# Causal softmax attention: scores from three float32r products of split queries and keys, and the weighted values moved ahead of the scores

## The chip, the cores and the metric

The kernel runs on one core of one Trainium2 chip. The metric is the device time of one execution in microseconds (us); lower is better. The engines of the core are named as the profile names them: PE (TensorE, the matmuls; PEld are its weight loads), DVE (VectorE), ACT (ScalarE), POOL (GpSimd) and SP (SyncE, which here only issues DMAs). Each engine has its own instruction stream and takes it in order; engines meet through semaphores.

## The reference, cut to what matters

Input x has 8 batches of 1024 tokens with 256 features. Four blocks follow one another, each with a layernorm in front and a residual around it: softmax attention, a feed-forward block, linear attention, the feed-forward block again. The change is in the first one alone:

```python
q = frac_rope(einsum('btm,mhd->bhtd', x, wq)) * D_HEAD ** (-0.5)   # 2 heads of 128
k = frac_rope(einsum('btm,mhd->bhtd', x, wk)) * D_HEAD ** (-0.5)
v = einsum('btm,mhd->bhtd', x, wv)
s = einsum('bhid,bhjd->bhij', q, k) - NEG * (i < j)
p = softmax(s, axis=-1)
o = einsum('bhij,bhjd->bhid', p, v)
return einsum('bhid,hdm->bim', o, wo)
```

`frac_rope` rotates the first 64 of the 128 features of a head (x times cos plus its swapped halves times sin) and leaves the others.

## The kernel before, in words

The attention phase (function `attention_phase`, from line 436) runs one batch after the other; `turn` of each engine is one batch. A batch is 8 blocks of 128 query rows and 2 heads, so 16 steps; step n works on block i = n // 2 and head h = n % 2, and its keys are the (i + 1) x 128 tokens up to the diagonal.

Number formats. A matmul with plain float32 operands is what the scores (line 832) and the weighted values (line 861) use; each such matmul shows in the trace as two MATMUL records. The projections (lines 322 and 331) and the output projection (line 872) use split operands: a float32r high part (a rounded copy) and a float32r low part (the rest), and three products of parts in place of one product.

The start of a batch. PE projects queries and keys for two halves of 512 tokens, m = 0 to 7 (line 322; m counts half, then query or key, then head). For each m, DVE multiplies by the cosine (`times_cos`, line 705) and ACT copies the swapped halves (`swap_halves`, line 648, two instructions). After every second m DVE multiplies the swapped copy by the sine (`times_sin`, line 712), and POOL adds the two (line 568). The rotary features of both heads lie so that POOL works on 64 partitions at a time; in the first half it does the first 128 tokens and the other 384 apart, queries and then keys. `first_rotated` counts the 128-token pieces, `rotated` the whole halves.

The 16 steps. `scores(n)` multiplies the block's queries with its keys in pieces of up to 512 keys and adds the causal mask on the diagonal (line 835). DVE takes the row maximum (`row_max`, line 722). ACT takes the exponentials (`exp_step`, line 622). PE transposes them in blocks of 128 x 128 (`transpose_probs`, line 850), ACT copies the transposes to SBUF (`evacuate_probs`, line 632), PE multiplies them with the values (`weighted_values`, line 861) into one PSUM bank O, ACT copies O rounded to float32r (`evacuate_out`, line 639), DVE writes the low part (`out_low`, line 717), PE projects (`out_projection`, line 872), DVE adds the result to x (`residual`, line 735). PE also projects the values of one block of 128 tokens at a time (`values`, line 331), which ACT copies (line 660).

The order of the work is written out by hand, one list for each engine. PE at step n: transposes of n, scores of n + 2, value projection of block n + 3, weighted values of n - 1, output projection of n - 2. ACT at step n: exponentials of n + 1, copies of the transposes of n, copy of the value block n + 3, copy of O of n - 1. DVE at step n: reciprocal of n, row maximum of n + 2, low part of O of n - 1, residual of n - 2, and at some steps a piece of the layernorm of the next batch (statistics at 4 and 6, line 131; normalising at 9 and 11, line 155). At steps 14 and 15, which have no scores n + 2, PE transposes the next batch's normalised input in eight matmuls (line 199), and DVE writes its low part (line 209).

There is one bank O. So `weighted_values(n)` waits until `out_low(n - 1)` has read it:

```python
pe.wait_ge(o_lo_done.sem, o_lo_done.at(b, n))      # line 859: n low parts written in this batch
```

Of the kernel before, what the change touches and what calls it, by code (L numbers as in the profile page):

```python
# [21 lines left out]
P = 128  # L22
NB, T, M = 8, 1024, 256
KT = M // P
# [411 lines left out]
def attention_phase(nc, block, sems, env, io, following, fronts, later):  # L436
# [6 lines left out]
    with ExitStack() as ctx:  # L443
# [18 lines left out]
        qk = sb("qk", [P, 2, HA, T])  # L462

        wqkv_raw = qk[:].rearrange("p s h t -> p (s h t)")[:, 0:KT * (WQK + HA * DA)].rearrange("p (k n) -> p k n", k=KT)
        swapped = sb("swapped", [P, NHALF * 2, UN])
        V = sb("v_a", [P, TB, HA * DA])

        steps = [(i, h) for i in range(TB) for h in range(HA)]
        NS = len(steps)
        prob = sb("prob", [P, 2, T])  # L470
        probT = sb("probT", [P, 2, TB, P])
# [4 lines left out]
        wo_raw = prob[:, 0, 0:HA * M].rearrange("p (h m) -> p h m", h=HA)  # L476
# [16 lines left out]
        rotated, first_rotated = sig("a_rotated", 2 * NHALF), sig("a_first_rotated", 2)  # L493
        v_ready, v_done = sig("a_v_ready", TB), sig("a_v_done", TB)
# [10 lines left out]
        def run_batches(eng, turn):  # L505
            turn(0, True, False)
            with eng.Fori(0, NB - 2) as p:
                turn(p + 1, False, False)
            turn(NB - 1, False, True)

# [36 lines left out]
        def _(pool):  # L547
            open_signals(pool, rotated, first_rotated)
# [6 lines left out]
            def turn(b, first, last):  # L555
# [5 lines left out]
                for half in range(NHALF):  # L561
                    for s in range(2):
                        pool.wait_ge(sin_done.sem, sin_done.at(b, 2 * half + s + 1))
                        for some in (slice(0, P), slice(P, UN)) if half == 0 else (slice(0, UN),):
                            for h in range(HA):
                                rows = slice(h * ROT, (h + 1) * ROT)
                                to = qk[rows, s, h, half * UN + some.start:half * UN + some.stop]
# [24 lines left out]
        def _(act):  # L592
# [3 lines left out]
            open_signals(act, swap_done, v_done, p_done, pt_done, o_hi_done)  # L596
# [53 lines left out]

            def square(part):
# [10 lines left out]
            def turn(b, first, last):  # L662
                for m in range(NPROJ - 1):
                    swap_halves(b, m)
                exp_step(b, 0)
                values(b, 0)
                swap_halves(b, NPROJ - 1)
                values(b, 1)
                for n in range(NS):
                    if n + 1 < NS:  # L670
                        exp_step(b, n + 1)
                    evacuate_probs(b, n)
                    if n == 0:
                        values(b, 2)
# [17 lines left out]
        def _(dve):  # L692
            for s in sx:
                s.dve_open(dve)
            open_signals(dve, cos_done, sin_done, o_lo_done, max_done, inv_done, y_done)
# [4 lines left out]
            def times_cos(b, m):  # L700
# [4 lines left out]
                nc.vector.tensor_tensor(qk[:, s, h, at], PS[:, PROJ_RING[m % 4], :], cos[:, h, at],  # L705
                                        ALU.mult).then_inc(cos_done.sem, 1)

            def times_sin(b, k):
# [4 lines left out]
                                        ALU.mult).then_inc(sin_done.sem, 1)  # L713

# [23 lines left out]
            def turn(b, first, last):  # L738
# [5 lines left out]
                for m in range(NPROJ):  # L744
# [5 lines left out]
                    if m == 1 and not first:  # L750
                        residual(b, -1)
                    if m % HA == 0 and m > 0:
                        times_sin(b, m // HA - 1)
                row_max(b, 0)
                row_max(b, 1)
                times_sin(b, NPROJ // HA - 1)
                for n in range(NS):
# [9 lines left out]
                    if not last:  # L767
# [3 lines left out]
                        if n in (9, 11):  # L771
                            ln.dve_normalise(dve, b + 1, (n - 9) // 2)
                    if n == 4 and last:
                        following.ln.dve_normalise(dve, 0)
# [41 lines left out]
        def _(pe):  # L816
# [4 lines left out]
            def scores(b, n):  # L821
                i, h = steps[n]
                if n == 0:
                    pe.wait_ge(first_rotated.sem, first_rotated.at(b, 2))
                elif n == HA or n == HA * UT:
                    pe.wait_ge(rotated.sem, rotated.at(b, 2 * (i // UT + 1)))
                keys = (i + 1) * P
                for c in range(0, keys, UN):
# [3 lines left out]
                    last = nc.tensor.matmul(bank[:, 0:w], qk[:, 0, h, i * P:(i + 1) * P], qk[:, 1, h, c:c + w],  # L832
                                            start=True, stop=not diag)
# [41 lines left out]
            def turn(b, first, last):  # L875
# [998 lines left out]
```

## Time and profile before

| | |
|---|---|
| time, median of 3 runs (lowest, highest) | 1889.74 us (1888.9, 1890.17) |
| span of the profiled execution | 1886.0 us |
| PE busy | 1843.9 us, 98% |
| DVE, ACT, POOL busy | 1395.0, 881.7, 589.6 us |

The profiled execution's own time is not listed beside its span. The span goes from the first to the last instruction, so the time is the span and a little around it: the median stands 3.74 us above the span. The busy time of PE counts overlapping records, so it says that PE was hardly ever without a matmul in flight, and not how fast it went; the distance from the start of one matmul to the start of the next says that. Attention takes the first 540 us of the span or so.

### The profile page before, as it was taken

The numbers are of one execution on the slowest core, as the hardware profiler recorded it, in microseconds if no ns is written. First come the engines' busy times: TensorE is split into PE (matmuls) and PEld (weight loads), VectorE is DVE, ScalarE is ACT, GpSimd is POOL, SyncE is SP. The second block draws the span as 40 slices with busy tenths as digits, with TensorE's granted clock in tenths as the row PEclk, the third lists the DMA queues.
The fourth block names the chain that finished last, engine by engine and source line by source line (L and its number), as shares of the span: only waits on it lengthen the run. The fifth ranks groups of instructions, "written<-read, shape, count | busy, mean of one in ns | idle before, by whom it ended". The sixth has DMA issues, their size and how long they took to land.

```text
span 1886.0 us, 36455 instructions
## 1 busy us (share of the span) xinstructions
PE 1843.9 (98%) x12481; PEld 1541.7 (82%) x12481; DVE 1395.0 (74%) x2679; ACT 881.7 (47%) x1717; POOL 589.6 (31%) x526
## 2 busy tenths in 40 slices
PE   8999999999999999999999999999999998999998
PEld 7888888888888888878787888788878877888887
DVE  6566566556668888777777878787878788888885
ACT  6656656665554444453333333333333332444443
POOL 5313203311332222233433333333333334522211
PEclk9999999999999999999999999999999999999999
DMA  7100000000022122120000000000000001222322
GB/s 246 43 1 0 0 0 0 0 0 0 13 54 54 29 33 32 29 62 13 13 12 12 11 11 11 11 11 11 11 11 11 12 12 20 38 62 62 65 55 58
DMA packets 230630, 53.19 MB, mean 28 GB/s; under 512 B 209696, under 2 KB 228768, under 8 KB 230176
## 3 DMA queue, kind: packets, MB, share of 16 engines
q1 hardware_dynamic: 229296, 49.53, 13.0%
q10 hardware_dynamic: 1264, 2.76, 0.4%
q8 instruction: 40, 0.66, 0.1%
q14 instruction: 30, 0.25, 0.0%
HBM read 18.69 MB, written 8.39 MB: 14 GB/s over the span
## 4 chain that ended last, share of the span: by engine, by line
PE 74%; DVE 9%; issue 6%; POOL 4%; SPq 2%; ACT 2%; DMA 1%; DVEq 0%; ACTq 0%; POOLq 0%
PE PS L1203 16%; PE PS L1212 9%; PE PS L322 8%; PE PS L331 7%; PE PS L861 7%; PE PS L832 6%; PE PS L850 3%; PE PS L1732 3%; PE PS L1706 3%; PE PS L1668 3%; SPq L270 2%; PE PS L1711 2%; PE PS L1721 2%; PE PS L872 2%; DVE lin_zq L1504 2%
## 5 line engine op out<-in xcount | busy, mean ns | idle before, releaser
L322 PE MATMUL PS<-ln_xh,lin_w 128*128 128x512 f32 x768 | 249.9, 394 | 9.2 <-POOL ln_xl L280 5.4
L1135 ACT ACTIVATE ff_silu<-PS 128x512 f32<-128x512 f32 x192 | 114.4, 597 | 232.9 <-PE PS L1203 204.5
L1170 DVE SCALAR_TENSOR_TENSOR ff_h<-PS,ff_silu 128x512 f32<-128x512 f32 x192 | 131.2, 684 | 107.7 <-PE PS L1203 94.1
L322 PEld LDWEIGHTS PS<-ln_xh,lin_w 128*128 128x128 f32 x768 | 144.3, 188 | 47.6 <-DVE lin_kT L1487 8.6
L568 POOL TENSOR_TENSOR qk<-qk,swapped 64x128 f32<-64x128 f32 (+2 forms) x96 | 96.9, 1009 | 240.2 <-DVE swapped L712 234.4
L1154 DVE TENSOR_TENSOR ff_h_lo<-ff_h,ff_h_hi 128x512 fp32r<-128x512 f32 x192 | 165.1, 860 | 0.4
L861 PE MATMUL PS<-probT,v_a 128*128 128x128 f32 x1152 | 153.3, 278 | 0.0
L861 PEld LDWEIGHTS PS<-probT,v_a 128*128 128x128 f32 x1152 | 139.5, 192 | 14.3 <-ACT probT L632 7.4
L322 PE MATMUL PS<-ln_xl,lin_w 128*128 128x512 f32 x384 | 150.2, 391 | 0.0
L832 PE MATMUL PS<-qk 128*128 128x512 f32 (+3 forms) x384 | 145.2, 489 | 1.0 <-POOL qk L568 0.9
L722 DVE TENSOR_REDUCE neg_max<-PS 128x1 f32<-128x256 f32 (+7 forms) x128 | 95.6, 752 | 62.3 <-PE PS L835 60.9
L166 POOL TENSOR_SCALAR ln_var_eps<-ln_mean_var 128x4 f32<-128x4 f32 x64 | 15.5, 242 | 402.7 <-DVE ln_mean_var L139 402.7
L1442 ACT ACTIVATE lin_yg_hi<-stage 128x512 fp32r<-128x512 f32 x64 | 40.3, 630 | 205.3 <-DVE stage L1550 135.1
L1121 ACT ACTIVATE ff_h_hi<-ff_h 128x512 fp32r<-128x512 f32 x192 | 119.5, 622 | 9.3 <-DVE ff_h L1170 9.3
L1418 POOL TENSOR_TENSOR lin_state<-lin_state,lin_decay_c 128x512 f32<-128x512 f32 x48 | 50.0, 1042 | 233.9 <-PE PS L1711 233.9
L1362 POOL TENSOR_TENSOR lin_qsT<-lin_qT,lin_decay_q 128x512 f32<-128x512 f32 x64 | 99.2, 1566 | 65.8 <-DVE lin_qT L1487 56.1
L1424 POOL TENSOR_TENSOR lin_yg_lo<-stage,lin_yg_hi 128x512 fp32r<-128x512 f32 x64 | 82.1, 1282 | 107.3 <-ACT lin_yg_hi L1442 107.3
L1457 ACT ACTIVATE ln_xn<-PS 128x512 f32<-128x512 f32 x128 | 76.6, 598 | 65.8 <-PE PS L322 56.7
L622 ACT ACTIVATE prob<-PS,neg_max 128x256 f32<-128x256 f32 (+7 forms) x128 | 94.4, 738 | 14.1 <-DVE neg_max L722 10.5
L1212 PE MATMUL PS<-ff_w_hi,ff_h_hi 128*128 128x256 f32 x384 | 97.7, 288 | 1.6 <-issue 1.4
L1212 PE MATMUL PS<-lin_w,ff_h_hi 128*128 128x256 f32 x384 | 97.6, 287 | 1.6 <-issue 1.5
L639 ACT ACTIVATE oT_hi<-PS 128x128 fp32r<-128x128 f32 x128 | 35.5, 277 | 135.1 <-PE PS L861 134.1
(190 smaller groups left out, 5354.2 us busy)
## 6 DMA issues: line engine op xcount, KB each, us to landing
ff_raw<-ln_xn SPq DMA_DIRECT2D x464, 32.0 KB, 2.0
ln_xl<-ln_xn SPq DMA_DIRECT2D x288, 32.0 KB, 2.0
out_x<-X SPq DMA_DIRECT2D x15, 512.0 KB, 2.9
X<-in_x SPq DMA_DIRECT2D x7, 1024.0 KB, 5.5
stage<-in_w_lin SPq DMA_DIRECT2D x1, 2048.0 KB, 8.1
stage<-in_w_gate SPq DMA_DIRECT2D x2, 768.0 KB, 7.4
stage<-in_w_up SPq DMA_DIRECT2D x2, 768.0 KB, 8.8
stage<-in_w_down SPq DMA_DIRECT2D x2, 768.0 KB, 10.2
```

The source lines that it names most:

```text
L322: last = nc.tensor.matmul(out, w, x, start=n == 0, stop=n == len(terms) - 1)
L331: last = nc.tensor.matmul(out, x[:, at], w, start=n == 0, stop=n == len(terms) - 1)
L568: done = nc.gpsimd.tensor_tensor(to, to, swapped[rows, 2 * half + s, some], ALU.add)
L832: last = nc.tensor.matmul(bank[:, 0:w], qk[:, 0, h, i * P:(i + 1) * P], qk[:, 1, h, c:c + w], start=True, stop=not diag)
L861: last = nc.tensor.matmul(O, V[:, j, h * DA:(h + 1) * DA], probT[:, n % 2, j, :], start=j == 0, stop=j == i)
L1121: nc.scalar.activation(h_hi[:, slot(par, f), :], h[:, f % 2, :], ACT.Copy).then_inc(hi_done.sem, 1)
L1135: nc.scalar.activation(silu[:, f % NB_GU, :], PS[:, f % NB_GU, :], ACT.Silu, scale=W_SCALE).then_inc(silu_done.sem, 1)
L1154: nc.vector.tensor_tensor(h_lo[:, slot(par, f), :], h[:, f % 2, :], h_hi[:, slot(par, f), :].bitcast(F32), ALU.subtract).then_inc(lo_done. ...
L1170: nc.vector.scalar_tensor_tensor(h[:, f % 2, :], PS[:, NB_GU + f % NB_GU, :], W_SCALE, silu[:, f % NB_GU, :], ALU.mult, ALU.mult).then_inc ...
L1203: ins = nc.tensor.matmul(PS[:, bank, :], w, x, start=n == 0, stop=n == len(parts) - 1)
L1212: ins = nc.tensor.matmul(Y[:, t // 2, (t % 2) * M:(t % 2 + 1) * M], a[:, slot(par, f), t * P:(t + 1) * P], w[:, f % NF, :], start=f == 0 a ...
L1362: nc.gpsimd.tensor_tensor(qsT[:, j, :].rearrange("p (c t) -> p c t", t=P), qT[:, j, :].rearrange("p (c t) -> p c t", t=P), Gq[:, j, :].uns ...
```

## The change

Queries and keys, once rotated, are split: ACT writes a float32r copy (`qk_hi`), DVE or POOL the float32r rest (`qk_lo`). Each piece of the scores is three float32r products in place of one float32 product. The work is cut by tokens: the first 128 of the first half (FIRST; low parts on DVE), its other 384 (REST; low part of the queries on POOL, of the keys on DVE), and the second half (WHOLE; both low parts on POOL). PE's list changes its order in two places: the first value projection comes ahead of the first two scores, and in each step the weighted values of n - 1 and the value projection come ahead of the scores of n + 2. To have room, the unsplit queries and keys live in the buffers of the probabilities and of the normalised input, and raw weights are loaded into the value buffer.

```diff
+        qk_hi, qk_lo = sb("qk_hi", [P, 2, HA, T], F32R), sb("qk_lo", [P, 2, HA, T], F32R)
+        qk = [prob[:].rearrange("p s (h t) -> p s h t", h=HA),
+              env["norm"].xn[:].rearrange("p t m -> p (t m)").rearrange("p (s h t) -> p s h t", s=2, h=HA)]
+        FIRST, REST, WHOLE = slice(0, P), slice(P, UN), slice(0, UN)
```

POOL, for each half, after its rotations:

```diff
-                pool.wait_ge(rotated.sem, rotated.at(b, 2 * NHALF))
+                    pool.wait_ge(rotated.sem, rotated.at(b, 2 * (half + 1)))
+                    for s in range(2):
+                        if half > 0 or s == 0:
+                            pool.wait_ge(qk_hi_done.sem, qk_hi_done.at(b, 2 * half + s + 1))
+                            some = WHOLE if half > 0 else REST
+                            nc.gpsimd.tensor_tensor(of_tokens(qk_lo, s, half, some), qk[half][:, s, :, some],
+                                                    of_tokens(qk_hi, s, half, some).bitcast(F32),
+                                                    ALU.subtract).then_inc(pool_lo_done.sem, 1)
+                    if half == 0:
+                        pool.wait_ge(pool_lo_done.sem, pool_lo_done.at(b, 1))
```

ACT, the copies and their places in the batch:

```diff
+            def qk_high(b, s, half, some):
+                ready, k, done = (first_rotated, s + 1, first_hi_done) if some == FIRST else (rotated, 2 * half + s + 1, qk_hi_done)
+                act.wait_ge(ready.sem, ready.at(b, k))
+                nc.scalar.activation(of_tokens(qk_hi, s, half, some), qk[half][:, s, :, some], ACT.Copy).then_inc(done.sem, 1)
...
                 for m in range(NPROJ - 1):
                     swap_halves(b, m)
+                    if m == 3:
+                        qk_high(b, 0, 0, FIRST)
+                    if m == 5:
+                        qk_high(b, 1, 0, FIRST)
+                        qk_high(b, 0, 0, REST)
+                values(b, 0)
+                qk_high(b, 1, 0, REST)
                 exp_step(b, 0)
-                values(b, 0)
                 swap_halves(b, NPROJ - 1)
                 values(b, 1)
                 for n in range(NS):
                     if n + 1 < NS:
                         exp_step(b, n + 1)
                     evacuate_probs(b, n)
+                    if n == 1:
+                        for s in range(2):
+                            qk_high(b, s, 1, WHOLE)
```

DVE:

```diff
+            def first_low(b, s):
+                dve.wait_ge(first_hi_done.sem, first_hi_done.at(b, s + 1))
+                nc.vector.tensor_tensor(of_tokens(qk_lo, s, 0, FIRST), qk[0][:, s, :, FIRST],
+                                        of_tokens(qk_hi, s, 0, FIRST).bitcast(F32), ALU.subtract).then_inc(first_lo_done.sem, 1)
...
+                    if m in (5, 6):
+                        first_low(b, m - 5)
...
                 row_max(b, 0)
                 row_max(b, 1)
+                rest_k_low(b)
                 times_sin(b, NPROJ // HA - 1)
...
                         if n in (9, 11):
+                            dve.wait_ge(pool_lo_done.sem, pool_lo_done.at(b, 3))
                             ln.dve_normalise(dve, b + 1, (n - 9) // 2)
```

PE, the waits, the products and the order:

```diff
                 if n == 0:
-                    pe.wait_ge(first_rotated.sem, first_rotated.at(b, 2))
-                elif n == HA or n == HA * UT:
-                    pe.wait_ge(rotated.sem, rotated.at(b, 2 * (i // UT + 1)))
+                    pe.wait_ge(first_lo_done.sem, first_lo_done.at(b, 2))
+                elif n == HA:
+                    pe.wait_ge(pool_lo_done.sem, pool_lo_done.at(b, 1))
+                    pe.wait_ge(rest_k_lo_done.sem, rest_k_lo_done.at(b, 1))
+                elif n == HA * UT:
+                    pe.wait_ge(pool_lo_done.sem, pool_lo_done.at(b, 3))
...
-                    last = nc.tensor.matmul(bank[:, 0:w], qk[:, 0, h, i * P:(i + 1) * P], qk[:, 1, h, c:c + w],
-                                            start=True, stop=not diag)
+                    for k, (q_part, k_part) in enumerate(((qk_hi, qk_hi), (qk_hi, qk_lo), (qk_lo, qk_hi))):
+                        last = nc.tensor.matmul(bank[:, 0:w], q_part[:, 0, h, q], k_part[:, 1, h, c:c + w],
+                                                start=k == 0, stop=k == 2 and not diag)
...
+                values(b, 0)
                 scores(b, 0)
                 scores(b, 1)
-                values(b, 0)
...
                     transpose_probs(b, n)
+                    if n + 2 >= NS and not last:
+                        sx[n + 2 - NS].pe(pe, b + 1, b + 1)
+                    if n >= 1:
+                        weighted_values(b, n - 1)
+                    if n == 0:
+                        values(b, 2)
+                    if n + 3 < TB:
+                        values(b, n + 3)
                     if n + 2 == HA * UT:
                         pe.wait_ge(v_done.sem, v_done.at(b, TB))
                     if n + 2 < NS:
                         scores(b, n + 2)
-                    if n == 0:
-                        values(b, 2)
-                    if n + 3 < TB:
-                        values(b, n + 3)
-                    if n + 2 >= NS and not last:
-                        sx[n + 2 - NS].pe(pe, b + 1, b + 1)
-                    if n >= 1:
-                        weighted_values(b, n - 1)
                     if n >= 2:
                         out_projection(b, n - 2)
```

## Rows read from the trace of the kernel before

**Rows 1.** The page: busy time of each engine; the chain that ended last, by engine.
```profile
PE 1843.9 (98%) x12481; PEld 1541.7 (82%) x12481; DVE 1395.0 (74%) x2679; ACT 881.7 (47%) x1717; POOL 589.6 (31%) x526
...
PE 74%; DVE 9%; issue 6%; POOL 4%; SPq 2%; ACT 2%; DMA 1%; DVEq 0%; ACTq 0%; POOLq 0%
```

**Rows 2.** One batch's stretch: us, busy PE, PEld, DVE, ACT, POOL, then PEclk.
```profile
223.56:289.18 65.62, 65.62 (x441) 55.34 (x440) 40.11 (x103) 39.62 (x99) 14.65 (x17) 1.00 0.00 0
```

**Rows 3.** Timeline of PE: start us, us, line, shapes; a distance between starts is the pace.
```profile
234.69 1.02 PE L832 MATMUL PS<-qk 128*128 128x512 f32 x2
235.55 0.22 PE L835 MATMUL PS<-mask_b,ident_b 128*128 128x128 bf16 x1
...
268.17 1.04 PE L850 MATMUL PS<-ident,prob 128*128 128x128 f32 x8
269.04 1.04 PE L199 MATMUL PS<-ident,ln_xn 128*128 128x128 f32 x8
...
283.74 0.39 PE L322 MATMUL PS<-a_xh,wqkv_hi 128*128 128x512 f32 x1
...
288.96 0.39 PE L322 MATMUL PS<-a_xh,wqkv_lo 128*128 128x512 f32 x1
...
290.08 0.28 PE L331 MATMUL PS<-wqkv_lo,ln_xh 128*128 128x256 f32 x1
290.20 0.28 PE L331 MATMUL PS<-wqkv_hi,ln_xh 128*128 128x256 f32 x1
```

**Rows 4.** Timeline of PE and of DVE late in a batch: mask, maximum, low part.
```profile
266.14 0.22 PE L835 MATMUL PS<-mask_b,ident_b 128*128 128x128 bf16 x1
266.19 1.78 PE L861 MATMUL PS<-probT,v_a 128*128 128x128 f32 x14
267.73 0.36 PE L872 MATMUL PS<-wo_a_hi,oT_hi 128*128 128x256 f32 x1
...
266.40 1.23 DVE L722 TENSOR_REDUCE neg_max<-PS 128x1 f32<-128x1024 f32 x1 [1.80 <-PE PS L835]
268.32 0.29 DVE L717 TENSOR_TENSOR oT_lo<-PS,oT_hi 128x128 fp32r<-128x128 f32 x1 [0.70 <-ACT oT_hi L639]
268.53 0.48 DVE L735 SCALAR_TENSOR_TENSOR X<-PS,row_inv,X 128x256 f32 x1
```

**Rows 5.** Groups by shape, DVE, 90 to 480 us: narrowest and widest maximum used below.
```profile
L722 DVE TENSOR_REDUCE neg_max<-PS 128x1 f32<-128x1024 f32 x12 | 14.7, 1224 | 14.1 <-PE PS L835 14.1
...
L722 DVE TENSOR_REDUCE neg_max<-PS 128x1 f32<-128x384 f32 x12 | 6.7, 558 | 2.1 <-PE PS L835 1.5
```

**Rows 6.** Timeline of PE: a value projection that waited for ACT's copy.
```profile
292.83 0.39 PE L331 MATMUL PS<-wqkv_hi,ln_xh 128*128 128x256 f32 x1
293.05 0.28 PE L331 MATMUL PS<-wqkv_hi,ln_xl 128*128 128x256 f32 x1
```

**Rows 7.** Timeline of POOL (twice, to different ends) and of ACT in a batch's start.
```profile
284.17 7.09 POOL L568 TENSOR_TENSOR qk<-qk,swapped 64x128 f32<-64x128 f32 x8 [37.76 <-DVE swapped L712]
...
284.17 12.82 POOL L568 TENSOR_TENSOR qk<-qk,swapped 64x128 f32<-64x128 f32 x12 [37.76 <-DVE swapped L712]
...
292.39 0.39 ACT L660 ACTIVATE v_a<-PS 128x256 f32<-128x256 f32 x1
...
295.48 0.27 ACT L639 ACTIVATE oT_hi<-PS 128x128 fp32r<-128x128 f32 x1
```

**Rows 8.** Groups by shape, 541 to 800 us: SBUF subtractions and a float32r copy elsewhere.
```profile
L1154 DVE TENSOR_TENSOR ff_h_lo<-ff_h,ff_h_hi 128x512 fp32r<-128x512 f32 x90 | 77.6, 862 | 0.1
...
L280 POOL TENSOR_TENSOR ff_odd_xl<-ff_raw,ff_odd_xh 128x1024 fp32r<-128x1024 f32 x8 | 19.4, 2428 | 43.4 <-ACT ff_odd_xh L275 43.4
...
L275 ACT ACTIVATE ff_odd_xh<-ff_raw 128x1024 fp32r<-128x1024 f32 x8 | 8.5, 1059 | 13.8 <-DMA ff_raw<-ln_xn 11.2 <-PE PS L1203 2.6
```

**Rows 9.** Timeline of PE in the linear attention; a stretch behind it (columns as rows 2).
```profile
838.37 0.88 PE L1678 MATMUL PS<-lin_zq,lin_head_sum 128*32 128x512 f32 x2 [3.44 <-issue]
...
840.00:841.00 1.00, 1.00 (x6) 0.83 (x3) 1.00 (x3) 0.00 (x0) 0.88 (x1) 0.50 0.00 0
```

More of the change, by code:

```diff
@@ L493, in attention_phase @@
         rotated, first_rotated = sig("a_rotated", 2 * NHALF), sig("a_first_rotated", 2)
+        qk_hi_done, first_hi_done = sig("a_qk_hi_done", 2 * NHALF), sig("a_first_hi_done", 2)
+        first_lo_done, rest_k_lo_done = sig("a_first_lo_done", 2), sig("a_rest_k_lo_done", 1)
+        pool_lo_done = sig("a_pool_lo_done", 3)
         v_ready, v_done = sig("a_v_ready", TB), sig("a_v_done", TB)
@@ L509, in run_batches, with of_tokens @@
             turn(NB - 1, False, True)
+        def of_tokens(parts, s, half, some):
+            return parts[:, s, :, half * UN + some.start:half * UN + some.stop]
         def score_rows(n):
@@ L547, in _ @@
         def _(pool):
-            open_signals(pool, rotated, first_rotated)
+            open_signals(pool, rotated, first_rotated, pool_lo_done)
             ln.pool_open(pool)
@@ L566, in turn @@
                                 rows = slice(h * ROT, (h + 1) * ROT)
-                                to = qk[rows, s, h, half * UN + some.start:half * UN + some.stop]
+                                to = qk[half][rows, s, h, some]
                                 done = nc.gpsimd.tensor_tensor(to, to, swapped[rows, 2 * half + s, some], ALU.add)
                             done.then_inc((first_rotated if some.stop == P else rotated).sem, 1)
-                pool.wait_ge(rotated.sem, rotated.at(b, 2 * NHALF))
+                    pool.wait_ge(rotated.sem, rotated.at(b, 2 * (half + 1)))
[8 more added lines that the diff above has]
+                        pool.wait_ge(pool_lo_done.sem, pool_lo_done.at(b, 1))
                 if first:
@@ L694, in _ @@
                 s.dve_open(dve)
-            open_signals(dve, cos_done, sin_done, o_lo_done, max_done, inv_done, y_done)
+            open_signals(dve, cos_done, sin_done, o_lo_done, max_done, inv_done, y_done, first_lo_done, rest_k_lo_done)
             ln.dve_open(dve)
@@ L704, in times_cos @@
                 dve.wait_ge(proj_ready.sem, proj_ready.at(b, m + 1))
-                nc.vector.tensor_tensor(qk[:, s, h, at], PS[:, PROJ_RING[m % 4], :], cos[:, h, at],
+                nc.vector.tensor_tensor(qk[half][:, s, h, :], PS[:, PROJ_RING[m % 4], :], cos[:, h, at],
                                         ALU.mult).then_inc(cos_done.sem, 1)
@@ L713, in times_sin, with rest_k_low @@
                                         ALU.mult).then_inc(sin_done.sem, 1)
+            def first_low(b, s):
+                dve.wait_ge(first_hi_done.sem, first_hi_done.at(b, s + 1))
+                nc.vector.tensor_tensor(of_tokens(qk_lo, s, 0, FIRST), qk[0][:, s, :, FIRST],
+                                        of_tokens(qk_hi, s, 0, FIRST).bitcast(F32), ALU.subtract).then_inc(first_lo_done.sem, 1)
+            def rest_k_low(b):
+                dve.wait_ge(qk_hi_done.sem, qk_hi_done.at(b, 2))
+                nc.vector.tensor_tensor(of_tokens(qk_lo, 1, 0, REST), qk[0][:, 1, :, REST],
+                                        of_tokens(qk_hi, 1, 0, REST).bitcast(F32), ALU.subtract).then_inc(rest_k_lo_done.sem, 1)
             def out_low(b, n):
@@ L1865 @@
     }
-    nc = bacc.Bacc("TRN2", target_bir_lowering=False, num_devices=1)
+    nc = bacc.Bacc("TRN2", target_bir_lowering=False, num_devices=1, dynamic_dma_scratch_size=1024)
     io = {}
```

9 lines of the change are left out of this document (5 added, 4 removed).

## The prediction

> **What bounds the kernel now.** The page comes first: PE is busy 98% of the span, and three quarters of the chain that ended last is PE [rows 1]. That chain is the list of what to shorten, but the busy figure says little of pace. So the second view is the table of stretches, cut from one batch's first scores to the next's: a batch takes 65.62 us, PE is busy in all of it, and neither DVE nor ACT reaches 41 us [rows 2]. The third is PE's timeline, read by the distance between starts: a batch is a dense row of matmuls, each kind at its own pace [rows 3]. In attention, PE's own work is therefore the time, and a microsecond in which PE waits is lost for good. The fourth is the timeline of the other engines, since they decide whether PE waits after the change.
>
> The sum is made against the span of 1886.0 us. The median of the runs is 3.74 us above it, which I take as what lies around the span, and I add the difference to 1889.74. 0.2% (3.8 us) is what a measurement of this kernel can tell from no change.
>
> **Part 1: three float32r products for one float32 product (PE).** A 512-key piece takes 235.55 - 234.69 = 0.86 us now, two records of 0.43. A float32r product of 512 columns takes 0.227: 24 of them stand in a row, the first at 283.74 and the last at 288.96, 23 distances in 5.22 us. One of 256 columns takes 0.12 [rows 3]. A batch has 12 pieces of 512 keys, 4 of 384, 4 of 256 and 4 of 128. Now, in proportion to columns: 0.86 x (12 + 3 + 2 + 1) = 15.5 us. After, with 0.173 for 384 columns (between the two rows): 3 x (12 x 0.227 + 4 x 0.173 + 4 x 0.12 + 4 x p) where p is the price of 128 columns, which no row has in float32r. From below, a quarter of the 512-column pace: 0.057. From above, as much as a whole float32 piece of 128 keys: 0.215. I take 0.11, the pace of the eight transposes, also 128 columns with one weight load each (0.87 / 8) [rows 3]. That gives 13.0 us, a gain of **2.5 us a batch** (1.2 to 3.1).
>
> The Trainium skill, "TensorE: Matmul & The Clock Gate", section "Back-to-back issue gap", gives about 131 ns for a 512-column matmul in a stream with weight loads; by that the gain would be about 3.5 us a batch more. The rows measure 0.227, so the sum keeps that.
>
> **Part 2: the start of a batch.** POOL adds the rotation without a break from 284.17, is through the first half at 291.26 and through the second at 296.99 [rows 7]. The change puts the subtraction for REST of the queries between the halves: 768 columns; the nearest row is 2.43 us for 1024, so 1.8 us [rows 8]. The second half is then rotated at 298.9. ACT, in step 1, waits for exactly this in the copy of WHOLE of the keys, about 1.06 us [rows 8], to 299.9. Behind it in ACT's queue stand the copy of value block 4 (0.39) and the copy of O of step 0 (0.27) [rows 7], to about 300.5; then DVE's low part (0.29 [rows 4]) and PE's restart. Weighted values of step 1 can start at 300.9. Now ACT makes this copy of O at 295.48 [rows 7].
>
> What has PE to do until then? The projections end at 289.19. In the new order come five value blocks (6 x 0.12 each, 3.6), four scores with masks (about 1.8), four transposes (0.44) and the weighted values of step 0 (0.22): 6.0 us, to 295.2. PE loses about **5.6 us a batch** (4.4 if that subtraction goes at DVE's pace [rows 8] and the two small copies are hidden; 6.6 if value block 4 reaches ACT a microsecond late). Smaller waits earlier (ACT's two REST copies push the first exponentials and the value copies back by some 2 us) lie inside this loss.
>
> **Part 3: the order in every step.** Weighted values of n need the low part of O of n - 1. DVE makes it behind the row maximum of n + 2, which waits for the scores of n + 2. Now those scores are followed by weighted values, output projection, transposes and the next scores before the low part is wanted. After the change only an output projection and the transposes of n + 1 lie between. Count from the start of the mask that ends the scores. DVE's maximum starts 0.26 later (266.14 to 266.40). It holds DVE for some 0.07 less than its duration, as the low part does: 0.29 long, and the next instruction starts 0.21 after it. Then comes the low part itself, 0.29 [rows 4]. A PE that waits restarts late: the copy ended at 292.78 [rows 7], the matmul opens at 292.83, and the next follows after 0.22 where 0.12 is usual [rows 6], so 0.15. With a maximum of 0.56 (384 keys, step 2) to 1.22 (1024 keys, step 12) [rows 5] that is 1.19 to 1.85. The cover is 0.05 for the mask (to 266.19), 0.44 for the output projection (267.73 to 268.17), and 0.11 for each transpose, 2 to 7 of them [rows 3, 4]: 0.71 to 1.26. PE waits 0.5 to 0.6 in the even steps and 0.1 less in the odd ones, which have one transpose more: 5.3 us for the 11 steps 2 to 12. In steps 13 and 14 the next batch's transposes cover it. The statistics that DVE does in steps 4 and 6 delay the next maximum; I add 0.4. **5.7 us a batch** (4.2 without the statistics and without the 0.1 by which a restarted PE is slower; 7.5 if every wait is longer by another 0.15, as much as the restart itself).
>
> **Edits that I cost at nothing.** FIRST: DVE's low part of the keys waits for ACT's copy, which waits for POOL's first 128 keys. These are instructions 5 and 6 of the 8 in 7.09 us, so done at about 288.7 [rows 7], and the low part a microsecond later; the first value block, moved there, covers it. If it did not, the loss would be part of part 2's wait. REST of the keys on DVE (768 columns at 0.86 per 512 [rows 8], 1.3 us) stands ahead of the last sine product and delays it by about 2 us; POOL wants that product only after the REST subtraction, and it comes in time. POOL's two WHOLE subtractions (2 x 2.43) end at about 303.8, some 4 us before the scores of step 8 would start now, and DVE's normalising in step 9 is later still. The raw weights are only loaded elsewhere: no DMA moves in its queue, SP's list is as before, and PE's wait for them still precedes the first value block. DVE gains some 2.1 us and ACT 4.5 us of work a batch, against some 25 us of idle time each [rows 2].
>
> **The sum.** -2.5 + 5.6 + 5.7 = +8.8 us a batch, with 8 batches +70: 1889.7 + 70 = **1960 us**. Lowest with all bounds: -3.1 + 4.4 + 4.2 = +5.5, so 1934. Highest: -1.2 + 6.6 + 7.5 = +12.9, so 1993.
>
> **The rivals.**
>
> *The products pay and the queues have slack.* If the low part of O came early enough in every step and the copy of O of step 0 were not late, only part 1 stays: -2.5 x 8 = -20, 1870 us, faster. For it: DVE, ACT and POOL idle a third of a batch or more [rows 2], and PE does not wait for them now. Against it: the place is a queue, not a load; DVE's list still has the maximum first. It decides where the waits add up to less than 2.5 us a batch. 7%.
>
> *One of the two waits is hidden.* With part 2 alone +3.1 a batch, 1914; with part 3 alone +3.2, 1915. For it, each wait rests on one chain of five or six rows. 8%.
>
> *The clock falls.* In the linear attention PE stood 3.44 us, and two microseconds after it had started again the granted clock stood at 0.50, 1.2 in place of 2.4 GHz [rows 9]. In part 2, PE's last wait is about as long, once a batch, if the earlier waits are small. If the clock stays there for as long as PE had stood, 3.4 us at half pace lose 1.7; 8 of them make 1960 + 14 = 1974. The skill's page named above says in "HAM oscillation" that idle gaps between bursts put the clock back to half rate; the row agrees for 3.44 us, and no row shows a shorter wait that did it. 17%.
>
> *The products run at the float32 pace.* Then three of 0.43 replace 0.86 and the scores cost 7.7 us a batch more in place of 2.5 less: about 2045. The projections' rows speak against it [rows 3]. 1%.
>
> **How the numbers follow.** The forecast has 67%, with 1934 to 1993 as its range. The fallen clock lies inside that range, so the range holds 84% as it stands and I leave it. Slower by over 0.2%: 67 + 17 + 8 + 1 = 93%, less 1 for a mixture that ends near zero: 92%. Faster: 6% of the 7 of the first rival; the remaining 2% within 0.2%.
>
> **What would show it right or wrong.** In the profile after: a batch some 9 us longer than 65.62; score records of 512 columns 0.23 apart; PE's weighted values waiting for DVE's low part in most steps, about 0.5 us each, and once a batch for over 3 us; ACT's copy of O of step 0 right behind the copy of WHOLE of the keys, and that one released by POOL. The forecast is wrong if the weighted values start without a wait, if the batch shrinks, or if 128-column products show a pace far from 0.11. Feed-forward and linear attention should not change.

## The result, and the profile after

The changed kernel takes **1994.51 us** (median of 4 runs, 1993.93 to 1996.11), the kernel before 1889.32 us beside it: a ratio of 1.0556, 95% interval [1.0544, 1.0569]. Slower, as forecast (92%); but 1960 us was forecast, and the range ended at 1993. The span of the profiled execution is 1993.3 us, 107.3 above that of before, and its own time 1995.07, 1.8 above its span. So of the 3.74 us that the forecast put around the span, some 2 were the difference between runs; since the forecast adds its change to the median, this moves nothing in it.

The page of the changed kernel answers to [rows 1]: busy time, chain, and the group of weighted values with its idle time.

```profile
PE 1873.9 (94%) x12673; PEld 1587.2 (80%) x12673; DVE 1424.1 (71%) x2703; ACT 921.2 (46%) x1765; POOL 646.1 (32%) x550
...
PE 50%; issue 22%; DVE 12%; POOL 8%; SPq 3%; ACT 2%; DMA 1%; DVEq 0%; ACTq 0%; POOLq 0%
...
L913 PE MATMUL PS<-probT,v_a 128*128 128x128 f32 x1152 | 162.3, 287 | 57.8 <-DVE oT_lo L759 57.7
```

PE's share of the chain fell from 74% to 50%, and one group of matmuls now has 57.8 us of idle time ahead of it, nearly all of it ended by DVE's low part of O. PE's waits from 150 to 480 us (a little over four batches; each line has the total in us, the number of times and the longest) show the pattern: a long one and a dozen short ones in each batch.

```profile
PE PS L913 <- DVE oT_lo L759: 30.7, 51, 3.8
PE PS L902 <- ACT prob L640: 4.2, 4, 1.1
PE PS L331 <- ACT v_a L683: 2.1, 4, 0.5
```

One batch as a stretch, and two single microseconds in it (columns as in [rows 2]):

```profile
338.86:417.34 78.48, 69.30 (x464) 60.82 (x464) 43.74 (x106) 44.63 (x105) 21.67 (x20) 0.96 0.00 0
...
350.00:351.00 1.00, 0.83 (x4) 0.86 (x5) 0.10 (x2) 0.43 (x3) 1.00 (x2) 0.50 0.00 0
...
356.00:357.00 1.00, 1.00 (x9) 0.84 (x9) 0.00 (x0) 0.49 (x2) 0.00 (x0) 0.99 0.00 0
```

A batch takes 78.48 us in place of 65.62 [rows 2], and PE's granted clock is no longer 1.00: it stands at 0.50 (1.2 GHz) for 6.8 us of the batch, from about 1 us before the long wait ends. The first two batches take 77.4 to 77.5, with 3.4 us at 0.50.

**The start of a batch** (projections end at 337.85), PE's timeline, then those of ACT, DVE and POOL:

```profile
341.71 0.33 PE L902 MATMUL PS<-ident,prob 128*128 128x128 f32 x1 [1.06 <-ACT prob L640]
...
343.26 0.39 PE L331 MATMUL PS<-wqkv_hi,ln_xh 128*128 128x256 f32 x1 [0.52 <-ACT v_a L683]
...
350.17 0.77 PE L913 MATMUL PS<-probT,v_a 128*128 128x128 f32 x2 [3.81 <-DVE oT_lo L759]
350.59 0.56 PE L331 MATMUL PS<-wqkv_hi,a_xh 128*128 128x256 f32 x1
350.95 0.41 PE L331 MATMUL PS<-wqkv_hi,a_xl 128*128 128x256 f32 x1
351.16 0.41 PE L331 MATMUL PS<-wqkv_lo,a_xh 128*128 128x256 f32 x1
```

```profile
345.79 1.05 ACT L672 ACTIVATE qk_hi<-ln_xn 128x1024 fp32r<-128x1024 f32 x1
348.21 1.06 ACT L672 ACTIVATE qk_hi<-ln_xn 128x1024 fp32r<-128x1024 f32 x1 [1.36 <-POOL ln_xn L577]
349.17 0.37 ACT L683 ACTIVATE v_a<-PS 128x256 f32<-128x256 f32 x1
349.44 0.27 ACT L657 ACTIVATE oT_hi<-PS 128x128 fp32r<-128x128 f32 x1
...
349.74 0.29 DVE L759 TENSOR_TENSOR oT_lo<-PS,oT_hi 128x128 fp32r<-128x128 f32 x1 [3.13 <-ACT oT_hi L657]
...
332.85 6.81 POOL L577 TENSOR_TENSOR prob<-prob,swapped 64x128 f32<-64x128 f32 x8 [40.18 <-DVE swapped L744]
339.73 2.15 POOL L584 TENSOR_TENSOR qk_lo<-prob,qk_hi 128x768 fp32r<-128x768 f32 x1
342.04 6.13 POOL L577 TENSOR_TENSOR ln_xn<-ln_xn,swapped 64x512 f32<-64x512 f32 x4 [0.16 <-POOL qk_lo L584]
```

This is the forecast chain link by link: POOL ends its rotations at 348.17, ACT's copy of WHOLE of the keys waits for that, the value block and O stand behind it, DVE follows, and PE starts at 350.17, 12.3 after its projections (forecast: 11.7). New is what comes after: a 256-column product goes at 0.21 us (350.95 to 351.16) in place of 0.12 [rows 3].

**A step**, PE's and DVE's timelines at full clock:

```profile
366.03 0.23 PE L887 MATMUL PS<-mask_b,ident_b 128*128 128x128 bf16 x1
...
366.50 0.60 PE L902 MATMUL PS<-ident,prob 128*128 128x128 f32 x4
367.46 1.13 PE L913 MATMUL PS<-probT,v_a 128*128 128x128 f32 x8 [0.36 <-DVE oT_lo L759]
368.35 0.48 PE L884 MATMUL PS<-qk_hi 128*128 128x512 f32 x1
368.66 0.39 PE L884 MATMUL PS<-qk_lo,qk_hi 128*128 128x512 f32 x1
368.89 0.39 PE L884 MATMUL PS<-qk_hi,qk_lo 128*128 128x512 f32 x1
369.12 0.22 PE L884 MATMUL PS<-qk_hi 128*128 128x128 f32 x1
...
366.29 0.82 DVE L764 TENSOR_REDUCE neg_max<-PS 128x1 f32<-128x640 f32 x1 [1.68 <-PE PS L887]
367.03 0.28 DVE L759 TENSOR_TENSOR oT_lo<-PS,oT_hi 128x128 fp32r<-128x128 f32 x1
```

The weighted values wait for a low part that stands behind the row maximum of the scores just made. The bracket says 0.36, counted from the modelled end of the last transpose (367.10). But four transposes at 0.11 [rows 3] let the next matmul start at 366.94, so 0.52 are lost.

**Where the 107.3 us are.** First scores come 1.2 later (27.2 for 26.1); the seven batches from first scores to first scores take 548.8 for 461.4, so 87.4; the last batch, to its last output projection, 10.5; and the three blocks behind the attention 8.5 to their last matmul (0.3 of it comes back behind that), in a dozen places of 0.3 to 1.5 us each.

### The profile page after: what moved, and what is told of

The parts are those of the page before. It is cut to its first block, busy times and chain, and to the rows that moved or that the text cites. A ratio compares the mean times of both kernels' runs of the same rounds, so it can differ in the third digit from the quotient of the medians.

```text
span 1993.3 us, 37046 instructions
## 1 busy us (share of the span) xinstructions
PE 1873.9 (94%) x12673; PEld 1587.2 (80%) x12673; DVE 1424.1 (71%) x2703; ACT 921.2 (46%) x1765; POOL 646.1 (32%) x550
## 3 DMA queue, kind: packets, MB, share of 16 engines
q1 hardware_dynamic: 229296, 49.53, 12.3%
## 4 chain that ended last, share of the span: by engine, by line
PE 50%; issue 22%; DVE 12%; POOL 8%; SPq 3%; ACT 2%; DMA 1%; DVEq 0%; ACTq 0%; POOLq 0%
PE PS L1255 14%; PE PS L1264 8%; PE PS L331 5%; PE PS L322 4%; SPq L270 3%; PE PS L913 3%; PE PS L1784 3%; PE PS L1758 2%; POOL prob L577 2%; PE PS L1763 2%; PE PS L1720 2%; PE PS L884 2%; PE PS L1773 2%; POOL ln_xn L577 2%; DVE ln_stats L131 2%
## 5 line engine op out<-in xcount | busy, mean ns | idle before, releaser
L913 PE MATMUL PS<-probT,v_a 128*128 128x128 f32 x1152 | 162.3, 287 | 57.8 <-DVE oT_lo L759 57.7
L577 POOL TENSOR_TENSOR prob<-prob,swapped 64x128 f32<-64x128 f32 (+1 forms) x64 | 51.0, 797 | 253.5 <-DVE swapped L744 249.9
L155 DVE TENSOR_SCALAR ln_xn<-X,ln_mean_var,ln_rstd 128x256 f32 (+1 forms) x256 | 97.3, 442 | 1.3 <-POOL ln_rstd L169 1.3
L1264 PE MATMUL PS<-ff_w_hi,ff_h_lo 128*128 128x256 f32 x384 | 95.9, 283 | 0.0
```

Of the source, the lines that this page charges most:

```text
L155: last = nc.vector.tensor_scalar(out, x, self.mean_var[:, t, 0:1], self.rstd[:, t:t + 1], ALU.subtract, ALU.mult)
L913: last = nc.tensor.matmul(O, V[:, j, h * DA:(h + 1) * DA], probT[:, n % 2, j, :], start=j == 0, stop=j == i)
L1264: ins = nc.tensor.matmul(Y[:, t // 2, (t % 2) * M:(t % 2 + 1) * M], a[:, slot(par, f), t * P:(t + 1) * P], w[:, f % NF, :], start=f == 0 a ...
```

## The experiments

Each ran beside the kernel before; its time is followed by the ratio to that kernel and the 95% interval. Each expectation, written ahead of its run, names a theory and a rival. Batch times and waits are those of the profiled execution. Unless said otherwise the diff is against the changed kernel.

**order_back: PE's steps in the order of before.**

```diff
                     transpose_probs(b, n)
-                    if n >= 1:
-                        weighted_values(b, n - 1)
...
                         scores(b, n + 2)
...
+                    if n >= 1:
+                        weighted_values(b, n - 1)
```

> The changed kernel with the old order of PE's steps (scores of n + 2 ahead of the value block and the weighted values of n - 1); the splits and all else stay. Theory (three losses: PE waits for the low part of O in every step, 5.5 us a batch; it waits once for 3.8 us at the start; the clock falls after that wait, 3.4 us a batch): the waits of the steps go, and at the start the scores of step 4 and value block 5 fill part of the long wait, so some 2.2 us of it are left. A batch then takes 66.5 to 67.5 us and the kernel 1897 to 1905 if the clock holds, about 1925 to 1930 if the shorter wait still brings it down. Rival (the order costs nothing, the float32r products and the splits do): above 1980, and the weighted values still wait in every step.

1923.09 us, 1.0183 [1.0166, 1.02], 2 us under the range that was given for a fallen clock. Batches with a full clock take 68.2. Its waits from 200 to 480 us, where the clock holds:

```profile
PE PS L913 <- DVE oT_lo L759: 8.5, 4, 2.1
PE PS L902 <- ACT prob L640: 4.3, 4, 1.1
PE PS L884 <- DVE qk_lo L754: 3.2, 4, 0.8
```

The dozen short waits are gone, and so is the fall of the clock in these batches; 10 us of each batch went with the two. Three waits at the start are left. The clock still fell in the first three batches and the last. So the order was the larger part. The first batch still took 75.0, which both_sq below was to mend.

**order_only: the kernel before with the new order alone, float32 scores** (the same lines moved the other way).

> The kernel before with nothing but the new order of PE's steps; scores stay float32, no splits. Theory: every step's weighted values wait for the low part of O behind the row maximum, 5.5 us a batch, and at the start some 1.5 us more; no wait is longer than 1 us, the clock holds. 71.5 to 73.5 us a batch, the kernel 1937 to 1952. Rival (the order is harmless by itself and the waits come from the added splits): 1885 to 1895.

1953.33 us, 1.0344 [1.0325, 1.0363], 1 us above the theory's range; the rival is out. Batches take 73.5, so the order alone loses 7.9. The clock never fell in them.

```profile
PE PS L861 <- DVE oT_lo L717: 16.2, 48, 0.6
PE PS L331 <- ACT v_a L660: 2.2, 4, 0.6
```

**low_first: DVE writes the low part of n - 1 ahead of the row maximum of n + 2.**

```diff
                     inverse(b, n)
+                    if n >= 1:
+                        out_low(b, n - 1)
                     if n + 2 < NS:
                         row_max(b, n + 2)
-                    if n >= 1:
-                        out_low(b, n - 1)
```

> The changed kernel with one swap on DVE: in each step the low part of O of n - 1 comes ahead of the row maximum of n + 2. PE's order stays new, the WHOLE copies stay in step 1. Theory: the waits of the steps come from the low part standing behind the maximum in DVE's queue, so they go (6.5 us a batch), while the long wait at the start and the fall of the clock after it stay: 71 to 73 us a batch, the kernel 1935 to 1952. Rival (the one bank O and PE's new order cause them whatever DVE does): 1985 or more.

1943.33 us, 1.0282 [1.0265, 1.0299]: hit. Batches take 71.8 to 71.9, 6.6 less than in the changed kernel. Up to 1 us of that may be the clock: three of these batches stand at half clock for 3.4 us in place of 6.8, and the changed kernel's batch with 3.4 takes 77.4. The rest, 5.5 or more, shows that it is the place in DVE's list, and neither DVE's load nor its durations, that makes PE wait in the steps.

**whole_late: ACT's two copies of WHOLE in step 3 in place of step 1.**

```diff
-                    if n == 1:
+                    if n == 3:
                         for s in range(2):
                             qk_high(b, s, 1, WHOLE)
```

> The changed kernel with ACT's two WHOLE copies in step 3 in place of step 1; PE's order stays new. Theory: the copy of O of step 0 no longer stands behind POOL, the 3.8 us wait shrinks below 1 us, the granted clock stays at full in the attention, the step waits of about 0.5 us stay. A batch loses 3 us of wait and 3.4 us of slow clock: about 72 us in place of 78.4, the kernel 1940 to 1948. Rival (the clock falls from the many small waits together, or for another reason): the clock still falls once a batch and only the 3 us go, 1965 to 1975.

1969.43 us, 1.0422 [1.0405, 1.044]. Batches take 75.1. The wait of 3.81 shrank to 0.58, which shows that it was ACT's queue; but the gain was 3.3 a batch, and the time lies in the rival's range, because the clock still fell, now only for 3.4 us. PE's waits and one microsecond of a batch:

```profile
410.43 0.32 PE L902 MATMUL PS<-ident,prob 128*128 128x128 f32 x1 [1.06 <-ACT prob L640]
...
411.98 0.42 PE L331 MATMUL PS<-wqkv_hi,ln_xh 128*128 128x256 f32 x1 [0.52 <-ACT v_a L683]
...
412.00:413.00 1.00, 1.00 (x5) 1.00 (x6) 1.00 (x1) 0.72 (x4) 0.94 (x2) 0.59 0.00 0
```

It stands at half already in 412 to 413, right behind two waits of 1.06 and 0.52.

**keep_busy: 30 products that nobody reads, in PE's list ahead of the long wait.**

```diff
+                    if n == 2:
+                        pe.wait_ge(y_done.sem, y_done.at(b, 0))
+                        for _ in range(30):
+                            nc.tensor.matmul(Y, sx[1].hi[:, 0, 0:P], sx[1].hi[:, 0, 0:M], start=True, stop=True)
                     if n >= 1:
                         weighted_values(b, n - 1)
```

> The changed kernel with 30 extra products of 256 columns (0.12 us each, 3.6 us) on PE ahead of the weighted values of step 1, into the bank of the output projection, whose contents nobody reads before it is written anew. Theory: the products fit into the wait of 3.8 us, which ends when it did; but PE does not stand still and the granted clock stays at full, so the 6.8 us at half clock go, 3.4 us a batch: 1966 to 1972. Rival (the clock is no price of its own, or falls anyway): 1990 to 2000, or up to 29 us more if the extra products lie on the path.

1981.04 us, 1.0486 [1.0469, 1.0504]: between the two ranges. The long wait's end, and a batch (columns as in [rows 2]):

```profile
341.52 3.83 PE L965 MATMUL PS<-a_xh 128*128 128x256 f32 x30
345.63 0.46 PE L913 MATMUL PS<-probT,v_a 128*128 128x128 f32 x2 [0.29 <-DVE oT_lo L759]
...
334.25:410.54 76.29, 70.33 (x495) 62.03 (x495) 43.67 (x106) 44.55 (x105) 21.79 (x20) 1.00 0.00 0
```

The weighted values start as late as before (11.4 after the first scores for 11.3), so only the clock differs. Batches without a fall take 76.2 to 76.4, against 78.4 with one of 6.8 us in the changed kernel: **the fall costs 2.0 us a batch**; the kernel gained 13.5. Three of its eight batches still have a fall of 3.4 us, begun ahead of the extra products, and take 76.8 to 77.4. The price is less than the theory had: the fall's first microsecond lies in the wait itself, and PE's slower work is cover for some of the step waits behind it.

**both_sq: order_back and whole_late together, and in the first batch the squares of the feed-forward weights two per step from step 12.**

> The changed kernel with three edits: PE's steps in the old order, the WHOLE copies in step 3, and ACT's squares of the first batch (they check the feed-forward weights) two a step from step 12 on, since POOL now prepares those weights later. Theory: no wait in the steps, no long wait at the start; left are the waits for the first exponentials and for the REST low parts, 2 to 3 us a batch, about as much as the products gain. 65.5 to 66.5 us a batch, the kernel 1886 to 1898; a fall of the clock in some batches adds little. Rival (the float32r scores cost more than the float32 ones): above 1910.

1916.6 us, 1.0145 [1.0128, 1.0162]: missed. Two batches, without and with a fallen clock:

```profile
239.19:305.06 65.87, 63.86 (x465) 58.17 (x465) 44.23 (x106) 43.74 (x105) 21.79 (x20) 1.00 0.00 0
305.06:372.45 67.39, 65.37 (x464) 59.64 (x464) 44.24 (x106) 43.72 (x105) 21.75 (x20) 0.97 0.00 0
```

Batches without a fallen clock take 65.87, 0.2 more than before, but most of them have 3.4 us at half clock and take 67.4. The waits of 1.06 (transposes, for ACT's first exponentials) and 0.81 (scores of step 2, for DVE's low part) stay in each; the same two waits are followed by a fall in some batches and not in others. And the first batch took 76.8.

**late_split: a version meant to win.** It is the kernel before, order and start included; the scores of steps 0 to 7 stay float32, and only those of steps 8 to 15, the long ones, are three products. ACT makes the high parts in steps 2 to 4 and POOL the low parts behind its rotations, so that they are there before step 8 asks for them; ACT's squares stand as in both_sq. As in the changed kernel, buffers are shared anew and `dynamic_dma_scratch_size` is 1024. From the diff against the kernel before, the products:

```diff
+                    if i < UT:
+                        last = nc.tensor.matmul(bank[:, 0:w], qf[:, 0, h, i * P:(i + 1) * P], qf[:, 1, h, c:c + w],
+                                                start=True, stop=not diag)
+                    else:
+                        q = slice((i - UT) * P, (i - UT + 1) * P)
+                        for k, (q_part, k_part) in enumerate(((q_hi, k_hi), (q_hi, k_lo), (q_lo, k_hi))):
```

> A version meant to beat both: PE's order and the start of a batch as in the kernel before, with float32 scores in steps 0 to 7 from a buffer of their own; only steps 8 to 15 use the three float32r products, so the splits (keys of both halves, queries of the second) are made by ACT in steps 2 to 4 and by POOL behind its rotations, before step 8 wants them; the squares as in the run of three edits. Theory: the pieces of steps 8 to 15 gain 1.8 us a batch and nothing waits: 63.6 to 64.2 us a batch, the clock holds, the kernel 1872 to 1880. Rival (any copy in ACT's queue or any work on POOL next to DVE costs PE a wait): 1889 or more.

1885.93 us, 0.998 [0.997, 0.9989]: missed by 6 us. The batches are as expected, 63.83 us, without a wait; the first, 71.99, is not: PE waits 4.8 us there for DVE.

**late_split2: the scales of the next layernorm ahead of POOL's long subtraction** (against late_split). In late_split's first batch DVE's normalising waited for POOL, whose 10 us subtraction of the feed-forward weights stood ahead of the scales that it needs (late_split, DVE):

```profile
61.22 1.38 DVE L155 TENSOR_SCALAR ln_xn<-X,ln_mean_var,ln_rstd 128x256 f32<-128x256 f32 x4 [6.76 <-POOL ln_rstd L169]
```

```diff
-                    nc.gpsimd.tensor_tensor(raw, raw, env["ff_w_hi"][:].bitcast(F32),
-                                            ALU.subtract).then_inc(env["ff_low"], 1)
...
                         ln.pool_rstd(pool, b + 1, half)
+                    if first:
+                        nc.gpsimd.tensor_tensor(raw, raw, env["ff_w_hi"][:].bitcast(F32),
+                                                ALU.subtract).then_inc(env["ff_low"], 1)
```

> The version meant to beat both, with one more edit: in the first batch POOL makes the layernorm's scales for the second batch ahead of its 10 us subtraction on the feed-forward weights, not behind it. Theory: in the run before, the first batch took 72.0 us in place of 63.8, since DVE's normalising in step 9 stood until POOL had come through those weights, and ACT and PE behind it (one wait of 4.8 us on PE). With the scales first that wait goes: the first batch 64 to 65.5 us, the kernel 1875 to 1880. Rival (the first batch's wait comes from the squares on ACT, or from something else): 1884 to 1888 as before.

1886.7 us, 0.9988 [0.9979, 0.9997]: missed; the first batch took 73.5. DVE no longer waits, but one of its rows is long. POOL's and DVE's timelines:

```profile
52.45 9.99 POOL L594 TENSOR_TENSOR stage<-stage,ff_w_hi 128x4608 f32<-128x4608 f32 x1
...
53.86 0.48 DVE L756 SCALAR_TENSOR_TENSOR X<-PS,row_inv,X 128x256 f32<-128x256 f32 x1
54.26 9.31 DVE L155 TENSOR_SCALAR ln_xn<-X,ln_mean_var,ln_rstd 128x256 f32<-128x256 f32 x4
63.49 0.15 DVE L748 RECIPROCAL row_inv<-row_sum 128x1 f32<-128x1 f32 x1
63.56 1.07 DVE L743 TENSOR_REDUCE neg_max<-PS 128x1 f32<-128x896 f32 x1
```

Four normalising instructions, 1.37 us elsewhere, take 9.31 and end 1.1 after POOL's one instruction. The first of them alone takes 8.34, to 62.60, where POOL ends at 62.44; the three others take their usual 0.4 each. So the first stood until POOL was through; DVE's row just before, with a PSUM operand, ran beside POOL in its usual 0.48.

**late_split3: that subtraction in two pieces, each behind a normalising** (against late_split2).

```diff
-                        nc.gpsimd.tensor_tensor(raw, raw, env["ff_w_hi"][:].bitcast(F32),
-                                                ALU.subtract).then_inc(env["ff_low"], 1)
+                        for j, part in enumerate((slice(0, 4 * WPART), slice(4 * WPART, NW))):
+                            pool.wait_ge(ln.ready.sem, ln.ready.at(b + 1, j + 1))
+                            nc.gpsimd.tensor_tensor(raw[:, part], raw[:, part], env["ff_w_hi"][:, part].bitcast(F32),
+                                                    ALU.subtract).then_inc(env["ff_low"], 1)
```

> The late split once more, with GpSimd's one 10 us subtraction of the first batch cut in two pieces (2048 and 2560 columns), each of them issued only when VectorE has normalised half of the next batch's input; ScalarE's squares of the later parts wait for the second piece. Theory (a long GpSimd instruction on SBUF holds up VectorE's normalising, which took 9.31 us beside it instead of 1.37): the four normalising instructions of the first batch are back near 1.4 us in sum, TensorE waits nowhere over 1 us in the first batch, the first batch takes 64 to 66 us and the kernel 1876 to 1880. Rival (the first batch is late for another reason): 1884 to 1888 again, with a wait of over 4 us left in it.

**1878.96 us, 0.9948 [0.9935, 0.9962]: 0.5% faster than the kernel before**, and the theory hit. DVE, POOL, and a stretch as long as a batch:

```profile
55.10 1.37 DVE L155 TENSOR_SCALAR ln_xn<-X,ln_mean_var,ln_rstd 128x256 f32<-128x256 f32 x4
...
56.55 4.57 POOL L596 TENSOR_TENSOR stage<-stage,ff_w_hi 128x2048 f32<-128x2048 f32 x1 [3.26 <-DVE ln_xn L155]
...
62.27 1.37 DVE L155 TENSOR_SCALAR ln_xn<-X,ln_mean_var,ln_rstd 128x256 f32<-128x256 f32 x4
...
63.72 5.67 POOL L596 TENSOR_TENSOR stage<-stage,ff_w_hi 128x2560 f32<-128x2560 f32 x1 [2.60 <-DVE ln_xn L155]
...
221.00:284.83 63.83, 63.83 (x458) 57.44 (x457) 39.96 (x102) 42.16 (x102) 21.69 (x20) 1.00 0.00 0
```

The first batch takes 64.7 and PE's longest wait in it is 0.6. So the products do pay, where PE's order and the start of a batch stay as they were.

## Why the prediction was wrong in its size

Direction and mechanisms held: the likeliest case came about, and all its waits are in the trace at their forecast places; but the fallen clock, which the prediction held to be a rival, came on top of it. The size was short, by terms of different weight. For a batch from the third on, in us:

```text
                         forecast   measured
products (part 1)          -2.5       -1.9
start of a batch (part 2)  +5.6       +6.3
order in the steps (3)     +5.7       +6.4
fallen clock                0         +2.0
sum                        +8.8      +12.8   (78.48 - 65.62 = 12.86)
```

**Part 1: right in pace, 0.6 too high in sum.** Columns go as forecast: 0.23 for 512 (368.66 to 368.89), 0.11 for 128. In order_back, 65.62 + 4.15 of waits (2.13, 1.06, 0.81 and 0.14) + 0.4 for PE's restarts - 68.22 leaves a gain of 1.9. The records agree: counted from start to start, the scores of one of its batches take 14.4 us for 15.6 before, the transposes 7.0 for 7.8 and the masks 0.9 for 0.7. The first of three products often takes 0.31 (368.35 to 368.66), which the sum lacks; but in order_back it also opens 0.03 behind the last transpose in place of 0.11, which gives that back, so the 0.6 lies in no single row. The Trainium skill, "TensorE: Matmul & The Clock Gate", section "Back-to-back issue gap", gives 131 ns for a matmul of 512 columns in a stream. The trace has 0.23, as the projections had it, and the measurement decides.

**Part 2: right, 0.7 short.** Nearly all of it lies with POOL: the REST subtraction took 2.15 for 1.8, the second half's rotation 6.13 for 5.7, with 0.16 of waiting between, less 0.3 in the first half. Behind it the links took 2.0, as forecast. (The 6.3 takes PE's work up to there at the forecast 6.0; the prediction's own 300.9 less 295.2 is 5.7 where it has 5.6.)

**Part 3: right, 0.7 short.** From the mask to DVE's maximum 0.26, as forecast (366.03 to 366.29); the low part ends at 367.31. Then the restart: the matmul opens 0.15 later, where the forecast had 0.05, and in order_only the records of the weighted values take 16.45 a batch for 15.34, 0.09 for each of 12 waits. So a restart costs 0.24, not 0.15: one microsecond a batch. Step 14, which was thought covered, waits as well (0.17). The 6.4 is order_only's 7.9 less the waits that belong to the start there (0.55 and 0.58, with their restarts about 1.5). The prediction's upper bound of 7.5 is 7.4 by its own counting, since eleven waits longer by 0.15 add 1.65.

**The clock: this is the step that failed.** The forecast has a wait "about as long" as the 3.44 us of [rows 9] in each batch, behind which that row shows the clock at 0.50, and yet makes the fall a rival of 17%. On the forecast's own numbers it belonged in the sum, where it stood at nothing; the runs show 2.0 us a batch. The rival's price of 14 us for the kernel came close to keep_busy's 13.5, in part by luck: it has 3.4 us at half pace and all of it lost, the trace has 6.8 of which a part costs nothing. The ground for doubt, that earlier waits might make the last one short, had no row behind it; whole_late shows that even without it the clock falls. With those 14 us in the sum, the forecast is 1974 and its range ends at 2007. The range as stated was passed by 1.5 us only: without the fall, or without the 8.5 us behind the attention, the time would have lain inside it.

**Edits costed at nothing.** FIRST was nearly hidden in the steady batches (a wait of 0.14 ahead of the first scores; 1.54 in the last batch, where the kernel before waits 0.91), the waits of 1.06 and 0.52 lie inside part 2's loss, as the prediction said, and SP's list played no part (PE's one wait for a DMA is 4.8 us at the very start, 4.9 in the kernel before). That feed-forward and linear attention do not change was wrong by 8.5 us in the profiled run. order_back has 6.4 there, late_split3 2.6, and order_only, whose buffers and number formats are those of before, 2.3; no experiment was made on it, and its cause stays open.

**The rivals.** Slack in the queues is out (order_only, order_back); one hidden wait is out, since undoing either part gains (order_back, whole_late); products at the float32 pace are out. Products at the float32 pace would have been 2042 by the prediction's terms, where it has about 2045. The first rival's hope was right in one point: what late_split3 adds to the lists of ACT and POOL fits into their slack, because it stands where PE does not come to wait for it.

## What to carry to other kernels

A cheaper instruction on the engine that is the bound pays only if its operands' preparation and its new place leave the other engines' lists in the order in which that engine asks; putting one list back (order_back) undid two thirds of this loss, and one line moved in another list (low_first) half of it. When a forecast wait is as long as one that the trace shows with a fallen clock behind it, put the clock into the sum. And look for the place where the new work fits with no wait at all: the products of the last eight steps alone (16 of a batch's 24 pieces of scores), made late, beat all of them made early.

## What the runs showed of the hardware that was not expected

**Short waits bring the clock down too, and not each time.** In whole_late it fell in each steady batch behind waits of 1.06 and 0.52; in both_sq, behind 1.06 and 0.81, in most but not in all; in order_only, with a dozen waits of up to 0.6 in a batch and one of 0.9 ahead of the last, never. It differs between executions too: the profiled one of whole_late took 1976.38 us at a mean granted clock of 0.988, the three others 1966 to 1970 at 0.991 to 0.994. The Trainium skill, "TensorE: Matmul & The Clock Gate", section "HAM oscillation", puts it down to long idle gaps between bursts; the runs agree that idle precedes each fall, but here gaps far below the 3.44 of [rows 9] did it. What tells the batches of both_sq apart stays open. A fall of 3.4 us cost 1.5 in both_sq, where nothing else waits, and 0.3 to 0.4 for one of 6.8 in order_back, where a wait was there anyway.

**One POOL instruction can hold up DVE for its whole length.** 9.31 for 1.37 us in late_split2, and gone in late_split3, which cuts POOL's instruction in two and lets each piece follow a normalising. The Trainium skill, "SBUF — State Buffer", section "Who interferes with whom", says that the two share a pair of ports, that an instruction like DVE's normalising can take both pairs, and that the second to come waits until the first is done; late_split2's rows agree: the second DVE instruction starts 0.1 us behind POOL's end. In the kernel before, the same subtraction ended ahead of the normalising, so the trap was not to be seen. Whether the last two sine products on DVE (1.48 and 1.55 us in the start of a batch after the change, 0.69 to 0.82 in that of before) stood for the same reason was not tried; POOL works beside them in both kernels.
